# First layer norm of batches 0 to 2 inside the attention steps, expert choice by groups of eight tiles, one-hots four at a time

## The reference

```python
def _layernorm(x, axis=-1, eps=1e-05):
    m = jnp.mean(x, axis=axis, keepdims=True)
    v = jnp.var(x, axis=axis, keepdims=True)
    return (x - m) / jnp.sqrt(v + eps)
...
    raw_gate = softmax(einsum('btd,de->bte', x, gate))
    _, topk_idx = top_k(raw_gate, 3)
    mask = one_hot(topk_idx, 16).sum(axis=2)
    gate_topk = mask * raw_gate / max(sum(abs(mask * raw_gate)), 1e-12)
    hidden = relu(einsum('btd,edh->bteh', x, W1) + b1)
    expert_out = einsum('bteh,ehd->bted', hidden, W2) + b2
    return einsum('bte,bted->btd', gate_topk, expert_out)
x = _layernorm(x + attention(x))
x = _layernorm(x + experts(x))
```

## Time and profile before

| | us |
|---|---|
| median of 3 runs | 1945.94 (1945.68 to 1947.75) |
| the profiled execution | 1947.0 |
| its span (what the profile shows) | 1945.0 |
| PE busy | 1733.5 (89%) |
| DVE busy | 1407.3 (72%) |
| POOL busy | 1178.5 (61%) |
| ACT busy | 761.3 (39%) |

### The profile page before, as it was taken

One profiled execution on the slowest core, in us unless ns is written; L12 is line 12 of the kernel. 1 busy time (PEld: TensorE's weight loads), 2 busy tenths in 40 slices (PEclk: granted clock), 3 DMA queues, 4 the chain that ended last, 5 costly groups with the idle time before them and its releaser, 6 DMA issues. The chain is left out here.

```text
span 1945.0 us, 33742 instructions
## 1 busy us (share of the span) xinstructions
PE 1733.5 (89%) x9679; PEld 1293.7 (67%) x9681; DVE 1407.3 (72%) x3369; ACT 761.3 (39%) x1691; POOL 1178.5 (61%) x1084
## 2 busy tenths in 40 slices
PE   5489999999999999999999999946779999999930
PEld 4357667667667667667767667523459999999930
DVE  3368888888888888888888888745974444444448
ACT  3134444454444444444444444416442222222226
POOL 2247777677677677678678678450335555555544
PEclk9689999999999999999999999978559999999975
DMA  9766457557567566557566556149002222222255
GB/s 316 260 192 188 143 172 212 153 172 208 156 177 209 153 180 202 158 174 202 167 171 202 149 166 182 34 158 370 15 20 71 70 70 70 70 70 70 70 187 184
DMA packets 164513, 300.97 MB, mean 155 GB/s; under 512 B 18768, under 2 KB 57360, under 8 KB 163360
## 3 DMA queue, kind: packets, MB, share of 16 engines
q1 hardware_dynamic: 152608, 269.79, 46.6%
q0 software_dynamic: 10752, 29.37, 4.8%
q10 hardware_dynamic: 1024, 0.26, 0.1%
HBM read 192.15 MB, written 106.95 MB: 154 GB/s over the span
## 5 line engine op out<-in xcount | busy, mean ns | idle before, releaser
L675 ACT ACTIVATE prob<-b_ps 128x512 f32<-128x512 f32 (+3 forms) x768 | 353.1, 488 | 361.6 <-PE b_ps L520 254.2
L447 POOL TENSOR_TENSOR acc<-acc,prob 128x1024 f32<-128x1024 f32 (+1 forms) x192 | 352.3, 1835 | 6.5 <-ACT prob L675 4.1
L420 POOL TENSOR_TENSOR roped<-rot 128x512 f32<-128x512 f32 x128 | 174.4, 1363 | 208.8 <-DVE rot L763 208.0
L519 PE MATMUL b_ps<-q,k 128*128 128x512 f32 (+3 forms) x768 | 294.8, 388 | 4.0 <-DMA q<-mrow 2.7
L512 PE MATMUL a_ps<-k,q 128*128 128x512 f32 (+3 forms) x768 | 264.9, 381 | 20.4 <-DMA k<-scratch_hilo 11.1
L745 DVE CUSTOM_DVE_ANT_0 masked<-a_ps,causal 128x128 bf16<-128x128 f32 (+3 forms) x512 | 237.8, 480 | 55.0 <-PE a_ps L512 45.5
L593 PE MATMUL y_ps<-prob,v_sb 128*64 128x512 f32 (+3 forms) x1536 | 273.8, 491 | 0.0
L520 PE MATMUL b_ps<-q,k 65*128 65x512 f32 (+3 forms) x768 | 264.0, 348 | 0.0
L1405 DVE TENSOR_SCALAR hT<-h_ps,b1T 128x128 f32<-128x128 f32 x448 | 126.1, 344 | 184.2 <-PE h_ps L1324 183.8
L789 DVE RECIPROCAL inv<-inv 128x128 f32<-128x128 f32 x256 | 232.2, 929 | 8.7 <-ACT inv L707 6.3
L425 POOL TENSOR_TENSOR lo<-roped,hi 128x512 fp32r<-128x512 f32 x128 | 177.5, 1387 | 83.9 <-ACT hi L688 83.9
(11 more groups left out here) (246 smaller groups left out, 2568.5 us busy)
## 6 DMA issues: line engine op xcount, KB each, us to landing
q<-scratch_hilo SPq DMA_DIRECT2D x192, 256.0 KB, 4.5
k<-scratch_hilo SPq DMA_DIRECT2D x192, 256.0 KB, 5.2
scratch_hilo<-hi SPq DMA_DIRECT2D x64, 512.0 KB, 4.1
scratch_hilo<-lo SPq DMA_DIRECT2D x64, 512.0 KB, 4.7
w_sb<-scratch_wsplit SPq DMA_DIRECT2D x32, 512.0 KB, 3.6
w<-in_L_ffn_W_dram SPq DMA_DIRECT2D x32, 512.0 KB, 10.3
got<-scratch_ys SPq DMA_DIRECT2D x32, 384.0 KB, 6.9
wv_sb<-scratch_wsplit SPq DMA_DIRECT2D x16, 512.0 KB, 6.2
```

The lines of the kernel that those rows point to most:

```text
L447: nc.gpsimd.tensor_tensor(sums, old, probs(q), ALU.add).then_inc(m["sum_p"], 1)
L519: nc.tensor.matmul(out, k1[s][:, h, js], q1[s][:, h, qs], start=True, stop=False, skip_group_check=True)
L675: nc.scalar.activation(probs(q)[:, h, :], b_ps[:, h, 0:w], ACT.Exp).then_inc(exp_done[h], 1)
```

## The change

- Attention: `bout` is finished in step 1 (two PE products into `y_ps`, one DVE add). POOL adds it to the residual rows of each batch, four operations of 128x512 per batch, as event `p0` at places 2 to 5 (batch 3 included). For batches 0 to 2, in the steps of the following batch: DVE takes moments of two tiles at events `z0` and `z1` of places 1 and 2; at `z0` of place 3 `scales` computes mean and inverse root by a chain of linked 128x8 operations (no Sqrt on ACT); ACT normalizes two tiles at each of `y0` to `y3` of place 4; SP stores 1 MB at place 5 and reloads at place 6.
- Routing: only batches 0 and 1 (2 MB) are loaded, in normalized form; 2 and 3 are in SBUF already; batch 3 alone is normalized here and stored (1 MB, still behind the weights on SP). The bias matrix of the experts is split in a high and a low part and multiplied in two products.
- The choice runs by groups of 8 tiles behind the logits (`choose`, `weigh`), in the order of batches 2, 0, 1, 3. The list of slots is computed with fewer operations.
- The inversion runs in 24 batches of four (ring of 3). DVE makes four tile one-hots in one operation of 448 elements and four row one-hots in one of 512, and in every third batch scales the tile one-hots by the row number; ACT makes the other coded copies (448 elements each); PE makes four products of 224 columns. 14 weighted biases are made before the loop, 13 in it from batch 3 on, 5 behind it.
- The scratch of the experts' outputs is laid out by choice first, which combine reads accordingly. The number of expert tiles is the same.

```diff
@@ -37,12 +37,12 @@
...
-ACT_ORDER = parse("""E0.0 E0.1 E1.0 E1.1 E2.0 w1 E2.1 E3.0 d1- h0++ N1- E3.1 E4.0 E4.1 h1++ E5.0 d0 h2++ E5.1 E6.0 N0 E6.1 E7.0
-w0+ E8.0 E7.1 h3++ E8.1 E9.0 E9.1 E10.0 v2++ E10.1 E11.0 E11.1 v3++""")
+ACT_ORDER = parse("""E0.0 E0.1 E1.0 E1.1 E2.0 w1 E2.1 E3.0 d1- h0++ N1- E3.1 E4.0 E4.1 y0 h1++ E5.0 d0 h2++ E5.1 E6.0 N0 E6.1 y1 E7.0
+w0+ E8.0 E7.1 h3++ E8.1 y2 E9.0 E9.1 y3 E10.0 v2++ E10.1 E11.0 E11.1 v3++""")
...
-M5.0+ r2++ G1- r3++ M5.1+ o1- M6.0+ R0 M6.1+ R1 M7.0+ R2 R3 G0 M7.1+ o2- M8.0+ M8.1+ M9.0+ o3- M9.1+ M10.0+
+M5.0+ r2++ G1- r3++ z0 M5.1+ o1- M6.0+ R0 M6.1+ R1 M7.0+ R2 R3 G0 z1 M7.1+ o2- M8.0+ M8.1+ M9.0+ o3- M9.1+ M10.0+
...
-POOL_ORDER = parse("""K11- T0 T1 T2 a0++ l0++ T3 a1++ l1++ a2++ l2++ K5 a3++ K6 l3++ K7 T8 T9 K8 T10 K9 T11 K10""")
+POOL_ORDER = parse("""K11- T0 T1 T2 a0++ l0++ T3 a1++ l1++ p0 a2++ l2++ K5 a3++ K6 l3++ K7 T8 T9 K8 T10 K9 T11 K10""")
...
+LN_STATS, LN_ROOTS, LN_APPLY, LN_STORE = 1, 3, 4, 5
...
+def inverse_root(V, link, variance, value, root, factor):
+
+
+    link(V.tensor_scalar(value, variance, EPS, None, ALU.add))
+    link(V.tensor_copy(factor, value.bitcast(I32)))
+    link(V.tensor_scalar(root.bitcast(I32), factor, -0.5, float(0x5F3759DF), ALU.mult, ALU.add))
+    for _ in range(3):
+        link(V.tensor_tensor(factor, root, root, ALU.mult))
+        link(V.tensor_tensor(factor, factor, value, ALU.mult))
+        link(V.tensor_scalar(factor, factor, -0.5, 1.5, ALU.mult, ALU.add))
+        link(V.tensor_tensor(root, root, factor, ALU.mult))
...
+            def store_x(b):
+
+                sp.wait_ge(m["normed"], TB * (b + 1))
+                sp.dma_start(xn[b], x1[:, b % 2 * TB:b % 2 * TB + TB, :]).then_inc(m["x_st"], 16)
...
+            for it in range(-2, STEPS):
+                turn(it, it)
+                b, place = it // PAIRS - 1, it % PAIRS
+                if b >= 0 and place == LN_STORE:
+                    store_x(b)
+                if 0 <= b < 2 and place == LN_STORE + 1:
+                    next_x(b)
...
+                    if kind == "p":
+                        rows = it % PAIRS - 2
...
+                        pool.wait_ge(m["bout_all"], 1)
+                        last = it - 1 if rows == 0 else it - 2
+                        pool.wait_ge(m["o_done"], 4 * last + rows + 1)
+                        two = x1[:, it // PAIRS % 2 * TB + 2 * rows:it // PAIRS % 2 * TB + 2 * rows + 2, :]
+                        nc.gpsimd.tensor_tensor(two, two, bout[:].rearrange("p (a d) -> p a d", a=1).broadcast_to([P, 2, D]),
+                                                ALU.add).then_inc(m["biased"], 1)
...
+                        if n == 1 and q == 1:
+                            pe.wait_ge(m["vo_done"], PAIRS)
+                            for h in range(2):
+                                ins = nc.tensor.matmul(y_ps[64 * h:64 * h + 64, 0:D], ones[:], vo[:], start=True,
+                                                       stop=True, skip_group_check=True)
+                            ins.then_inc(m["bout_sum"], 1)
...
+                        if n == 0 and q == 0:
+                            pe.wait_ge(m["bout_all"], 1)
...
+                    elif kind == "y":
+                        b = it // PAIRS - 1
+                        if b < 0 or b == B - 1 or it % PAIRS != LN_APPLY:
+                            continue
+                        act.wait_ge(m["ln_ready"], b + 1)
+                        for i in (2 * q, 2 * q + 1):
+                            row = x1[:, b % 2 * TB + i, :]
+                            nc.scalar.activation(row, row, ACT.Identity, bias=ln[3][:, i:i + 1], scale=ln[1][:, i:i + 1])\
+                                .then_inc(m["normed"], 1)
...
+            def moments(b, u):
+
+                dve.wait_ge(m["o_done"], 4 * PAIRS * (b + 1))
+                if u == 0:
+                    wait_for(dve, m["normed"], TB * b, b - 1)
+                for i in (2 * u, 2 * u + 1):
+                    ins = nc.vector.bn_stats(stats[:, i, :], x1[:, b % 2 * TB + i, :])
+                ins.then_inc(m["ln_stat"], 1)
+                if u:
+                    averages(b, u - 1)
+
+            def scales(b):
+                value, root, factor, shift = (part[:] for part in ln)
+                link(averages(b, 3))
+                inverse_root(nc.vector, link, mv[:, :, 1], value, root, factor)
+                nc.vector.scalar_tensor_tensor(out=shift, in0=mv[:, :, 0], scalar=-1.0, in1=root, op0=ALU.mult,
+                                               op1=ALU.mult).then_inc(m["ln_ready"], 1)
...
+                    if kind == "z":
+                        b, place = it // PAIRS - 1, it % PAIRS
+                        if b < 0 or b == B - 1:
+                            continue
+                        if LN_STATS <= place < LN_STATS + 2:
+                            moments(b, 2 * (place - LN_STATS) + q)
+                        elif place == LN_ROOTS and q == 0:
+                            scales(b)
...
+                        if n == 1 and q == 3:
...
+                            nc.vector.tensor_tensor(bout[:], y_ps[:, 0:D], bout[:], ALU.add).then_inc(m["bout_all"], 1)
...
+        HOT = 4
+        BATCHES = TOPK * TILES // HOT
+        PLACES_HOT = 3
+        BIASES_BEFORE, BIASES_AT_END, BIASES_FROM = 14, 5, 3
...
+        GROUP_ORDER = (2, 0, 1, 3)
...
+        def part_by_dve(a):
+            return a % 3 == 0
+
+        def biases_after(a):
+
+            if a == BATCHES - 1:
+                return range(TILES - BIASES_AT_END, TILES)
+            t = BIASES_BEFORE + a - BIASES_FROM
+            return range(t, t + 1) if BIASES_BEFORE <= t < TILES - BIASES_AT_END else range(0)
...
-            for b in range(B):
-                sp.dma_start(x1[:, b * TB:(b + 1) * TB, :],
-                             dram["xacc"][b].rearrange("p (t d) -> p t d", t=TB)).then_inc(x1_in[b], 16)
+            xn = dram["xn"].rearrange("(b t p) d -> b p t d", b=B, p=P)
+            for b in range(2):
+                sp.dma_start(S["x1a"][:, b * TB:(b + 1) * TB, :], xn[b]).then_inc(x1_in[b], 16)
             sp.dma_start(b1row[:], A["b1"]).then_inc(m["r_small"], 16)
...
-            for i in range(4):
-                sp.dma_start(b2r[32 * i:32 * i + E_, :], A["b2"]).then_inc(m["r_b2"], 16)
+            for i in range(P // E_):
+                sp.dma_start(b2_raw[E_ * i:E_ * (i + 1), :], A["b2"]).then_inc(m["r_b2"], 16)
             for e in range(E_):
...
-            xn = dram["xn"].rearrange("(t p) d -> p t d", p=P)
-            for g in range(0, TILES, LG):
-                sp.wait_ge(m["r_x1"], g + LG)
-                sp.dma_start(xn[:, g:g + LG, :], x1[:, g:g + LG, :]).then_inc(m["r_stored"], 16)
-            sp.wait_ge(m["r_stored"], 16 * TILES // LG)
-            sp.wait_ge(m["r_b2"], 64)
+            sp.wait_ge(m["r_x1"], LG)
+            sp.dma_start(xn[B - 1], S["x1b"][:, TB:2 * TB, :]).then_inc(m["r_stored"], 16)
+            sp.wait_ge(m["r_stored"], 16)
...
-            pool.wait_ge(m["r_stored"], 16 * TILES // LG)
...
+            pool.wait_ge(m["r_stored"], 16)
             for t in range(TILES):
                 pool.wait_ge(m["r_bb_sb"], t + 1)
-                nc.gpsimd.tensor_tensor(x1[:, t, :], biases[:, t % 2, :], x1[:, t, :], ALU.add)\
+                nc.gpsimd.tensor_tensor(token_rows(S, t), biases[:, t % 4, :], token_rows(S, t), ALU.add)\
                     .then_inc(m["r_bbadd"], 1)
...
-            for t in range(EARLY_BIASES):
+            for t in range(BIASES_BEFORE):
                 weighted_biases(t)
...
+            for a in range(BATCHES):
+                pe.wait_ge(m["r_row"], a + 1)
+                pe.wait_ge(m["r_part"], a + 1)
+                pe.wait_ge(m["r_code"], a + 1)
+                for b in range(HOT):
+                    c0 = b % 2 * 2 * SLOT_TILES
+                    ins = nc.tensor.matmul(tr_ps[:, b // 2, c0:c0 + 2 * SLOT_TILES], row_hot[:, a % PLACES_HOT, b, :],
+                                           coded[:, a % PLACES_HOT, b].rearrange("p v c -> p (v c)"),
+                                           start=(a == 0 and b % 2 == 0), stop=(a == BATCHES - 1),
+                                           skip_group_check=True)
+                ins.then_inc(m["r_inv"], 1)
+                if a == 2:
+                    count_begun()
+                for t in biases_after(a):
+                    weighted_biases(t)
...
+            for a in range(BATCHES):
+                s = a % PLACES_HOT
+                act.wait_ge(m["r_tile"], a + 1)
+                if a >= PLACES_HOT:
+                    act.wait_ge(m["r_inv"], a - PLACES_HOT + 1)
+                nc.scalar.activation(coded[:, s, :, 1, :], tile_hot[:, s], ACT.Copy, scale=float(a + 1))\
+                    .then_inc(m["r_code"], 1)
+                if not part_by_dve(a):
+                    act.wait_ge(m["r_part"], a)
```

(63 more changed lines are left out.)

483 lines of the change are left out of this document (213 added, 270 removed).

## The result

The changed kernel is slower: 1954.6 us, median of 5 runs (1953.2 to 1955.9), against 1945.7 (1945.0 to 1947.8) for the kernel before, ratio 1.0046 with a 95% interval of 1.0032 to 1.0060. Measured again later, beside 17 runs of before, it had 1954.9 and a ratio of 1.0036 (1.0022 to 1.0050). 1940.5 was forecast, in a range of 1919 to 1962.

The account below looks back on a forecast made before the run. PE was taken to set attention's pace, and routing to be a chain with no engine full. 1947.0 (profiled) - 41.8 (routing) + 36.5 (attention) = 1941.7; the unchanged median lies 1.1 lower, giving 1940.5, range 1919 to 1962.

Parts of the forecast that it names:

- the time given back: Attention: a step starting late is not idle for its usual 0.9 us; half of it, in 12 steps, returns 5.4 us.
- the stores and reloads put at nothing: Attention: SP's stores and reloads move to other places with the same bytes, so they cost nothing.
- Routing: Routing phase: earlier start, choice and slots, then a loop held by a store; lists ready 41.8 us sooner.
- the wait for the store: Routing loop: POOL's bias adds wait for the store behind SP's weights, begin at about 1348.4; DVE stands until 1356.9.
- The chain: Place 3, `z0`: DVE's root links wait for POOL's operations, PE stands and its clock falls; 10.6 us, three times, 31.8.
- B: Place 3: small links get the ports between or beside POOL's operations; 11 us instead of 31.8, time 1920; chance 0.17.
- D: Place 3: POOL does not run dry, so every link waits for it; 28 us more, time 1969; chance 0.12.
- ACT's normalizing: Place 4: row pairs between exponentials that PE waits for, 0.9 at `y1`, 0.65 at `y2`; 4.5 us for three batches.
- The moments: Places 1 and 2: BN_STATS and BN_AGGR at `z0`, where slack is nil, 0.75 + 1.0 us, three times: 5.1 us.
- a pace in the other steps that is not 36.7: Attention's other 29 steps: a PE pace other than 36.7 us would make all of the prediction wrong; no size given.
- Steps 0 and 1: Attention, step 1: the two products and the add of `bout` cost 0.5 us.
- 0.02 of slower within the forecast: Whole kernel: the forecast case had chance 0.46, split into 0.27 faster, 0.17 within 3.9 us of 1945.9, 0.02 slower.

Follow-up runs that it names:

- Run 3: Changed kernel, with POOL's bias adds in routing waiting for the store of normalized rows only from tile 24 on: 1946.8 us, ratio 0.9997 to before.
- run 1: Changed kernel without the 15 links of the inverse root in attention (batches 0 to 2; their normalized rows are wrong): 1925.1 us, ratio 0.989 to before.
- run 7: Changed kernel with the same 16 links on DVE moved to place 4, ahead of the first rotary product: 1939.1 us, ratio 0.9946 to before.
- run 4: Changed kernel with the root's chain on POOL at place 4, and normalizing, store and reload one place later: 1929.7 us, ratio 0.990 to before.
- run 8: Changed kernel with the chain in two parts on POOL, normalizing, stores and reloads later, bias adds gated from tile 24 on: 1907.4 us, ratio 0.977 to before.
- Run 5: Changed kernel with the store of batch 2 waiting for the first residual add of the last step: 1951.1 us, ratio 1.0012 to before.
- run 6: Run 5's kernel, with ACT normalizing one tile at a time over places 4 and 5, stores and reloads at 6 and 7: 1945.1 us, ratio 0.9975 to before.
- run 9: Run 8's kernel, with ACT normalizing one tile at a time over places 5 and 6, store and reload both at place 7: 1904.0 us, ratio 0.977 to before.
- run 2: Changed kernel with the store of batch 2 moved from place 5 to place 7 of the last batch, without a wait: 1953.0 us, ratio 1.0030 to before.

## Why the prediction was wrong

It said faster by 5 us, and the kernel is slower by 7 to 9. Two large terms of opposite sign stand in the sum, both right within 1.1 us, and the small ones beside them decided the sign. Two steps of the working failed most: the time given back, and the stores and reloads put at nothing.

- *Routing*: 41.8 forecast, 41.5 measured; start, choice, slots, the wait for the store, 1.2 us of comparisons a batch with POOL's half microseconds on top, and the decoding each within 2 us (the choice against the earlier of its two bounds). Run 3 confirms the wait.
- *The chain*: 31.8 forecast, 30.7 measured. The mechanism is as told: four links wait for POOL's operations, POOL runs dry on ACT's high half, the rest run at 0.2 (traces; runs 1 and 7). Rivals B and D fall. PE stood 8.3 us, 9.1 forecast, and ran at half rate for about 3.4.
- *ACT's normalizing*: 4.5 and 4.5. Run 1 shows that it isn't the chain's backlog, and in runs 4 and 8 it moves with ACT's events to the next place.
- *The moments*: 5.1 forecast, 1.3 measured against the usual step. The 1.7 us a batch were charged in full, on the ground that there was no slack. There was some: before, X0 starts 0.27 us behind the end of `o1`, now, where it waits, 0.05. With about 0.7 and 0.9 us of moments on DVE, `o1` comes 0.5 and 0.6 us late, X0 0.3 and 0.4, and the step is 0.16 and 0.26 longer.
- *Given back*, the first step that failed: -5.4 forecast, nothing measured. No step behind a stall is shorter than the usual 36.67; what comes back is 0.1 us inside the step itself (X0 0.29 late, the step 0.16 longer). A reading that fits, argued and not tested: the 0.9 us of PE's idle time in a step are waits inside it, which start over with each step however late it began.
- *"SP's stores and reloads come at other places with the same bytes: nothing"*, the second and larger: 6.8 us measured, 2.0 at places 5 and 6 and 4.8 in step 31. The prediction counted bytes, and not who is served behind the 1 MB: in step 31 ACT's transfer of 4 KB, at place 5 SP's own load of `xT`, and PE waits for both. Run 5 takes the 4.8 back by a later store, run 6 the 2.0 by another place. The prediction named this sign itself in its last sentence, a pace in the other steps that is not 36.7, but gave it no price.
- *The tail*: 3.2 us more, by 6.9 us at half clock, from 1294.2 to 1301.1. The changed kernel had it in both profiles (44.7 and 44.6 us from the last row maximum to the end) and so had run 9 (44.8); before and runs 1 to 8 did not (41.2 to 42.0). So it is neither the chain nor the early store that decides. PE's waits in front of it are the same as before, 0.91 and 0.22 us. What does decide is open.
- Steps 0 and 1 came 1.7 us late, but in all twelve profiles their end lies between 149.6 and 156.0 without a relation to the edits: 0.5 forecast, not to be settled.

In sum -5.4 became 0, 6.8 and 3.2 were not there, 3.8 and 1.1 were too much: 10.5 us. With 1.2 more in the first steps and 0.4 less in the others that makes 11.3, the gap between 36.5 and 47.8.

The stated range held the time, but by no merit of the sum: its own range was 1932 to 1950, attention's 28 to 42, and both were passed. That own range was too narrow even by its bounds, since 28 to 42 of loss and 36 to 50 of gain reach from 1924 to 1952. And with two terms near 40 that differ by 5, an error of a few microseconds in the small ones turns the sign; 0.02 of slower within the forecast, and 0.26 in all, were too little for that.
